# Attention's outputs cut into half rounds: twelve of sixteen array tiles in products of 128 columns, the four on the diagonal in 256

## The reference

```
q = gelu(x @ Wq + bq) + 0.21
k = gelu(x @ Wk + bk) + 0.21
v = x @ Wv + bv
q_r, k_r = rope(q), rope(k)            # x*cos + rotated(x)*sin
z   = 1 / (q . mean(k) + 1e-6)         # per head and token
kv  = k_r^T v / n                      # per head, 16 x 16
out = (q_r @ kv) * z                   # per head and token
return layernorm(out + x)
```

## Time and profile before

| | |
|---|---|
| median of 3 runs | 1833.14 us (1832.21 to 1834.62) |
| the profiled execution's own time | 1829.56 us |
| its span, first to last instruction | 1827.8 us |
| mean granted TensorE clock | 0.998 |
| PE busy | 1806.2 us, 99% of the span |
| PE's share of the chain that ended last | 96% |
| PE weight loads and matmuls | 19196 of each |

### The profile page before, as it was taken

One profiled execution on the slowest core, in us unless ns is written; L12 is line 12 of the kernel. 1 busy time (PEld: TensorE's weight loads), 2 busy tenths in 40 slices (PEclk: granted clock), 3 DMA queues, 4 the chain that ended last, 5 costly groups with the idle time before them and its releaser, 6 DMA issues.

```text
span 1827.8 us, 46210 instructions
## 1 busy us (share of the span) xinstructions
PE 1806.2 (99%) x19196; PEld 1477.8 (81%) x19196; DVE 1455.7 (80%) x3454; ACT 936.8 (51%) x1741; POOL 1016.6 (56%) x775
## 2 busy tenths in 40 slices
PE   9999999999999999999999999999999999999998
PEld 3336888888888888888887988888888888888887
DVE  3667787888888888888888768888888888888887
ACT  5554776677667776677667742222322232323231
POOL 1557998999999999999985012222222222222221
PEclk9999999999999999999999999999999999999999
DMA  8372210100103210000105931010101010101000
GB/s 294 150 268 111 94 60 3 37 2 2 37 2 106 94 37 3 29 10 3 60 3 197 306 101 35 36 35 29 42 24 47 24 47 24 46 24 44 26 12 24
DMA packets 25234, 115.38 MB, mean 63 GB/s; under 512 B 4480, under 2 KB 5440, under 8 KB 19904
## 3 DMA queue, kind: packets, MB, share of 16 engines
q1 hardware_dynamic: 21104, 89.69, 14.0%
q0 software_dynamic: 1152, 12.58, 2.0%
q10 hardware_dynamic: 2768, 10.15, 1.5%
HBM read 80.95 MB, written 31.46 MB: 62 GB/s over the span
## 4 chain that ended last, share of the span: by engine, by line
PE 96%; DVE 2%; ACT 1%; DMA 1%; issue 1%; POOL 0%; ACTq 0%; SPq 0%; DVEq 0%; POOLq 0%
PE bankC L1450 13%; PE bankC L32 7%; PE bankC L33 7%; PE bankC L34 7%; PE ring L32 6%; PE ring L34 6%; PE ring L33 6%; PE bankC L1449 6%; PE big L934 5%; PE big L34 3%; PE big L33 3%; PE big L32 3%; PE ring L866 3%; PE big L846 3%; PE conv_ps L256 3%; PE hid_ps L245 3%
## 5 line engine op out<-in xcount | busy, mean ns | idle before, releaser
L1450 PE MATMUL bankC<-down,act_hi 128*128 128x512 f32 x992 | 353.1, 397 | 0.0
L1449 PE MATMUL bankC<-down,act_lo 128*128 128x256 f32 x868 | 246.2, 284 | 0.0
L1450 PEld LDWEIGHTS bankC<-down,act_hi 128*128 128x128 f32 x992 | 186.3, 188 | 41.9
L1575 DVE TENSOR_TENSOR act_lo<-gel,act_hi 128x512 fp32r<-128x512 f32 x256 | 210.5, 822 | 8.7
L33 PE MATMUL bankC<-aT_lo,up_hi 128*128 128x512 f32 x512 | 199.6, 390 | 0.0
L32 PE MATMUL bankC<-aT_hi,up_hi 128*128 128x512 f32 x512 | 199.5, 390 | 0.0
L34 PE MATMUL bankC<-aT_hi,up_lo 128*128 128x512 f32 x512 | 199.4, 389 | 0.0
L1529 POOL TENSOR_TENSOR hC<-hC,vecC 128x1024 f32<-128x1024 f32 x16 | 38.7, 2416 | 282.9 <-PE turn L1424 282.9
L1535 POOL TENSOR_TENSOR rstdC<-var_epsC,minus_halfC 128x4 f32<-128x4 f32 x47 | 56.1, 1193 | 249.5 <-DVE var_epsC L1603 249.5
L1449 PEld LDWEIGHTS bankC<-down,act_lo 128*128 128x128 f32 x868 | 164.1, 189 | 1.4
L774 POOL TENSOR_TENSOR kr<-kr,kc 128x512 f32<-128x512 f32 x128 | 161.9, 1299 | 0.0
(11 more groups left out here) (215 smaller groups left out, 5262.3 us busy)
## 6 DMA issues: line engine op xcount, KB each, us to landing
raw_late<-in_AB SPq DMA_DIRECT2D x30, 320.0 KB, 4.0
u<-hA SPq DMA_DIRECT2D x8, 1024.0 KB, 5.0
u_next<-u SPq DMA_DIRECT2D x8, 1024.0 KB, 6.0
hC<-u SPq DMA_DIRECT2D x16, 512.0 KB, 4.0
xC<-in_x SPq DMA_DIRECT2D x16, 512.0 KB, 4.8
out<-w_flat SPq DMA_DIRECT2D x15, 512.0 KB, 2.6
w_flat<-in_AB SPq DMA_DIRECT2D x22, 320.0 KB, 3.7
w_split<-w_parts ACTq DMA_DIRECT2D x4, 1536.0 KB, 5.9
```

The costliest lines, as they stand in the source:

```text
L1449: e.matmul(bank[:, 0:H], a_lo[:, fb, tok], both[k][:, fb, 0, :], start=False, stop=False)
L1450: m = e.matmul(bank[:, :], a_hi[:, fb, tok], both[k][:, fb, :, :].rearrange("p a h -> p (a h)"), start=fb == 0, stop=fb == FB - 1)
L1575: e.tensor_tensor(a_lo[:, fb, :], g, a_hi[:, fb, :].bitcast(F32), ALU.subtract).then_inc(s_act_lo, 1)
```

## The change

Each tile off the diagonal (i not equal to j, 12 tiles) now takes its 256 columns in two halves of 128 (4 of the 8 token blocks each), so it has 8 products in place of 4. The four tiles on the diagonal keep products of 256 columns. The order becomes 8 half rounds of 14 products: k counts the channel half and the half of the columns, `part` the operand pair; in each half round the 12 tiles off the diagonal take one half product each, and two of the diagonal ones (i = 0, 1 in part 0; i = 2, 3 in part 1) a whole one. The waits ahead, the semaphore at the end and everything else stay.

```diff
-                for db in range(CB):
-                    for wt, q in ((kv, qc), (kv_rot, qs)):
+                def product(i, j, db, q, blocks):
+                    ch, wt = slice(D * i, D * i + D), kv if q is qc else kv_rot
+                    out = big[i][D * j:D * j + D, :].rearrange("p (a d c) -> p a d c", a=TILES, d=CB)
+                    return e.matmul(out[:, blocks, db, :], wt[ch, db, :], quarter(q[ch, db, :], j)[:, blocks, :],
+                                    start=q is qc, stop=q is qs)
+
+                whole, halves = slice(0, TILES), (slice(0, TILES // 2), slice(TILES // 2, TILES))
+                for k in range(2 * CB):
+                    for part in range(2):
                         for j in range(QUARTERS):
                             for i in range(GR):
-                                ch = slice(D * i, D * i + D)
-                                out = big[i][D * j:D * j + D, :].rearrange("p (a d c) -> p a d c", a=TILES, d=CB)[:, :, db, :]
-                                m = e.matmul(out, wt[ch, db, :], quarter(q[ch, db, :], j), start=q is qc, stop=q is qs)
+                                if i != j:
+                                    m = product(i, j, k // 2, (qc, qs)[part], halves[k % 2])
+                                elif i // 2 == part:
+                                    m = product(i, j, k // 2, (qc, qs)[k % 2], whole)
                 m.then_inc(s_out, 1)
```

## The result

The changed kernel took 1916.74 us (median of 4 runs, 1913.67 to 1918.13), the kernel before 1833.31 us beside it: 1.0452 times as long, 95% interval 1.0439 to 1.0464. That is slower, as forecast, but 27.7 us above the 1889 predicted and 8.7 us above the top of the range.

The account below looks back on a forecast made before the run. TensorE (PE), busy in 99% of the span, was taken as the bound: 1829.6 - 2.9 (array) + 67.4 (pauses) - 8.0 (today's pauses) = 1886.1 us, with 3.6 for the median 1889. Range 1834 to 1908 us.

Parts of the forecast that it names:

- the array time: TensorE's work in each unit's outputs without pauses: 2.6 us against 2.69 before, -2.9 us over 32 units.
- the feed: Issue rate in the outputs: 17.5 ns a product; 0.14 us for the first 32 loads, 1.68 us for 192.
- a wait of one short pass: Outputs: 0.11 us where a tile is met still busy, from part 0 to part 1; four give 2.77 us.
- tail: End of the outputs, from the last load to the keys' turn: 0.51 us a unit.
- The rival with a wait at every half round: Outputs: packets in time, eight waits of 0.11 us, 3.21 us a unit; +16.6 us, 1849.7 us, chance 0.05.
- the supply of instructions: Outputs and just behind: TensorE pauses at packet ends for the next packet, 2.1 us per unit, 67.4 us in all.
- ends that move slowly through the outputs: Expected in the profile: pauses a whole number of packets apart, shifting from unit to unit, 1.5 to 2.3 us each.
- one of my signs of being wrong: Outputs: packets usable sooner than 2.4 us after they begin would show the prediction wrong.
- the pull between the two terms: Outputs: a slower array reaches the packet's end later, so high array time and high pauses don't add fully.
- my uncut upper sum of 1918: Whole kernel: array at 2.6 us a unit with pauses at their 96 us bound; then cut to 1908.
- Packets in time: Outputs: three rivals without packet pauses, only array time changes: 1821.6, 1835.7, 1849.7 us; chances 0.12, 0.06, 0.05.
- The 25 ns between matmul starts: Skill page's minimum spacing, applied to the outputs: 224 matmuls take 5.6 us a unit, sum +93 us.

Follow-up runs that it names:

- a_early: Changed kernel with `turn_kv(n-1)` two projections earlier on PE and its copy ahead of `measure` on VectorE; 1890.14 us, 1.0307 times the kernel before.
- a_short: Changed kernel with the first channel half alone and its diagonal products cut to 128 columns; 1801.21 us.
- u_half: Changed kernel with one channel half alone and all 16 tiles, diagonal too, in 128 columns by rounds of 16; 1820.28 us.
- b_swap: Kernel before with rounds reordered: both channel halves with `kv`, then both with `kv_rot`; 1834.23 us, 0.9998 times the kernel before.
- pad: Kernel before with 48 products of 32 columns, later written over, ahead of each unit's 64; 1919.26 us.
- the early moves: `turn_kv(n-1)` two projections earlier on PE, its copy ahead of `measure` on VectorE: changed kernel 1890.14 us, kernel before 1828.66 us.
- pad16: Kernel before with 16 products of 32 columns, later written over, ahead of each unit's 64; 1854.38 us.

## Why the prediction was wrong in size

**The step that failed: the array time.** The text took 2.6 us a unit, with 3.21 as the high end, from the feed and a wait of one short pass wherever a busy tile is met. It is 4.02 us, shown in 13 units of `a_early`. In the prediction's own terms: first loads and feed 1.97 us in place of 0.14 + 1.68, tail 0.51 as assumed, and gaps of 1.54 us in place of 0.27. So the term is (4.024 - 2.686) x 32 = +42.8 us, not -2.9. The changed kernel's own trace bears this out up to its pauses. The mistake lies in how were read. Bursts of 32 and 2 loads every 0.645 us were put down to the tile that is met again, and the wait was then scaled by tile and spacing. The runs show that it comes after 34 loads with rounds of 14 as with rounds of 16 (`a_short`, `u_half`), and that it does not care for the order of the sums (`b_swap`). A block of 17 products of 128 columns takes 0.434 us, where the feed that I counted gives 17 x 17.5 ns = 0.30 us, and eight long products mixed among 48 short ones cost 0.51 us on top, 0.21 of it in the tail. The rival with a wait at every half round had the direction, with 16.6 us in place of 42.8, and not the place: the gaps don't stand at the half rounds.

**Right: the supply of instructions, in kind.** 24 more packets, 175 in all; a gap in every unit; ends that move slowly through the outputs; the full clock; PE above 90% of the chain; 50.5 us of "issue" on the loads, for which I had said some 50. (The 19 beside it was misread: 19.4 us count loads and matmuls, the loads alone had 14.5.) `pad` shows that instructions alone do it, and the early moves that what delays a packet is TensorE standing before the outputs: with the wait over sooner the packets begin sooner, the kernel before loses 8 of 8 pauses, and 13 units of the changed one are free of any. From a packet's start to the load that ends the pause the changed kernel takes 2.2 to 2.9 us, 2.4 in the median; sooner than 2.4 us was one of my signs of being wrong, and 22 of the 35 pauses show it, by 0.2 us at most. The sentence of the Trainium skill that the next block's fetch is mostly hidden ("Runtime: NRT & Kernel Launch", "Instruction fetch mechanics") fails once more for these bursts: in the changed kernel no unit's outputs hide it, with 35 pauses in 32 units. For the program as a whole, with 175 packets, it may well hold.

**In size, that term came out smaller, and not by my reasoning.** Pauses within outputs are 176.4 - 128.8 = 47.7 us, against 67.4, so net of the 8.0 of before +39.7 where I had +59.4. The array is slower than assumed and reaches a packet's end later, which I had named as the pull between the two terms. But `pad` shows that the forecast's size would have been short for a quick array: with some 3.5 us of array time it loses (180.1 - 3.5 x 32)/32 = 2.1 us a unit, a little of it to the clock, as much as I gave a unit of 2.6 us. The two terms depend on each other; with 448 instructions behind the held packet their sum is 5.5 to 5.6 us in both kernels, where I had 2.6 + 2.1 = 4.7. This is why the total, too, was above the range. Set against the profiled execution (1886.1 forecast, 1916.45 measured), the array term was 45.7 us short and the pauses 19.7 us too long; that they are of opposite sign, and that my uncut upper sum of 1918 would have held the time, is luck.

**The sum as measured**: 42.8 (array) + 39.7 (pauses) + 2.7 (behind the outputs) + 1.5 (later start of the first outputs) + 0.1 = 86.8 us, the difference of the spans. The medians differ by 83.4, since the profiled execution of before was a low one.

**The rivals.** Packets in time (1821.6, 1835.7 and 1849.7 us) is excluded by the 83.2 us of "issue". The 25 ns between matmul starts that the Trainium skill states ("TensorE: Matmul & The Clock Gate", the section on 56 against 53.3 ns) would have given +93 us and came near the +83.4 of the medians, but for a wrong reason: within the bursts of `u_half` loads start every 0.34/34 = 10 ns, and 13 units of `a_early` do in 4.02 us what would take 5.6 us by it.

**What stays open.** Why 17 products are a block, and by which rule two lengths make bursts of 34, 10, 22 and 12 loads; the runs show that for one length neither the spacing nor PSUM's sums explain it, and that of the 0.30 us which long ones cost between the products 0.24 go away when they stand at the end of each half round and 0.03 when they stand ahead. And how long `pad` would take with packets in time was worked out from `pad16` and from the units of `pad` that pause late, not measured in a whole unit.

## What to carry to other kernels

Splitting a product in two doubles what the sequencer has to fetch and issue for it: count instructions per stretch before columns. Where PE has to stand on a semaphore before a dense burst of small products, the next packet of its program is held back too: in these kernels it could be used only 2.9 us or more after the burst began, and a burst that came to its packet's end before that ran dry. The cure that worked was to release that wait earlier; reordering the burst (`b_swap`) did nothing for the pauses. When a trace shows bursts and gaps, test whether the gap follows the tile, the round or the plain count, with a kernel in which these three differ.

## What the runs showed of the hardware

- fp32 products of one length on 32 by 32 tiles go in blocks of 17 (34 loads): 0.645 us for 256 columns in rounds of 16, 0.434 us for 128 in rounds of 16 and of 14.
- Eight long products among 48 short ones: 2.21 us in their place, 1.98 at the end of each half round or ahead, 1.70 cut to the short length. The tail behind the last load is 0.51 us for a long product and 0.30 for a short one.
- A packet that is held up by a wait ahead of the outputs can be used 2.9 us or more after they begin (before, `u_half`, changed kernel), whatever the array does meanwhile. With 448 PE instructions the outputs take 5.5 to 5.6 us on average with array work of 3.5 or of 4.0 us.
- Releasing one wait earlier lets the packet begin 1.7 to 1.9 us ahead of the outputs instead of 0.5 to 0.7 us behind their start. All eight pauses go, and the kernel before is faster, 0.9974 (0.9964 to 0.9985), although the stretch between two units' outputs grows by 0.12 us.
- Behind the three longest pauses of `pad` (2.6 to 2.9 us without a load) the granted clock fell to 1.2 GHz for 3.4 us. In the changed kernel's outputs it stayed full.
